# A metaformer block on one core: weights loaded by themselves, a first group in halves, uses placed one place later, scaling moved, and a last norm in four pieces

## What is computed

```python
x = x + conv_ref(_ln_c(x), w1, b1, w2, b2, w3, b3)
t = x.reshape(16, 1024, 128)
t = t + ffn_ref(_ln_t(t), W_gat, att_src, att_dst, ..., edge_index)
# conv_ref(A): three scans, each rewrites channels of A in place
#   4 steps:  A[..., 32 i : 32 i + 32] = conv1x1(A, w1) + b1;      then relu
#   4 steps:  A[..., 32 i : 32 i + 32] = conv3x3(A, w2) + b2;      then relu
#   128 steps: A[..., i] = conv1x1(A, w3) + b3;                    returns A + its input
# ffn_ref: h = x @ W_gat; attention of the nodes over 524,288 edges and its softmax give each
#   token scores; the best two of four experts (gelu networks) are summed with softmax weights
```

## Time and profile before

| | us |
|---|---|
| median of 3 runs | 2232.84 (2232.25 to 2235.68) |
| the profiled execution | 2235.35 |
| its span in the trace | 2233.7 |
| busy: PE, DVE, ACT, POOL | 1096.8, 1750.7, 772.6, 1183.2 |
| DVE busy in 75 to 470 | 387.65 of 395 |
| DVE busy in 550 to 575 | 1.40 of 25 |

### The profile page before, as it was taken

The page is one execution under the profiler, slowest core; times in us unless marked ns, Lnnn a source line. Parts: engine busy times, 40 slices in busy tenths (PEclk is TensorE's granted clock), DMA queues, the critical chain, the costliest instruction groups (busy, mean ns, idle before and its releaser), DMA issues. The chain is left out here.

```text
span 2233.7 us, 17018 instructions
## 1 busy us (share of the span) xinstructions
PE 1096.8 (49%) x4914; PEld 492.8 (22%) x4914; DVE 1750.7 (78%) x3468; ACT 772.6 (35%) x1293; POOL 1183.2 (53%) x1167
## 2 busy tenths in 40 slices
PE   3886887688678899301601243332424242415230
PEld 1223343333454333100200021111102020202010
DVE  5999999998649999999383555868685859595868
ACT  4663854635245555200300133222323131313121
POOL 2000000000047777777776777777777777777760
PEclk9898877878569999755855676676767575757665
DMA  8301131021455222211231234352524342524251
GB/s 290 134 1 39 38 8 38 1 8 39 45 43 99 73 73 71 52 15 41 76 45 13 39 104 123 74 165 62 174 64 156 83 156 68 171 67 157 67 147 56
DMA packets 142649, 177.40 MB, mean 79 GB/s; under 512 B 64154, under 2 KB 115292, under 8 KB 132956
## 3 DMA queue, kind: packets, MB, share of 16 engines
q1 hardware_dynamic: 86988, 88.84, 14.4%
q0 software_dynamic: 40768, 42.44, 12.0%
q10 hardware_dynamic: 14800, 45.04, 5.2%
HBM read 99.82 MB, written 76.40 MB: 79 GB/s over the span
## 5 line engine op out<-in xcount | busy, mean ns | idle before, releaser
L534 POOL DMA_INDIRECT KC<-node_dram,KB x1026 | 1051.3, 1025 | 939.9 <-DMA node_dram<-node_out 627.5
L757 PE MATMUL hidden_out<-XT,W 128*128 128x512 f32 x512 | 291.9, 677 | 552.3 <-ACT ARENA_A L977 551.4
L762 PE MATMUL hidden_out<-ARENA_A,W 128*128 128x512 f32 x512 | 267.2, 648 | 24.9 <-ACT ARENA_A L977 24.9
L977 ACT ACTIVATE ARENA_A<-hidden_out,b1c 128x512 f32<-128x512 f32 x256 | 174.2, 687 | 246.1 <-PE hidden_out L757 245.5
L757 PEld LDWEIGHTS hidden_out<-XT,W 128*128 128x128 f32 x512 | 98.9, 214 | 702.5 <-ACT ARENA_A L977 581.2
L1052 ACT ACTIVATE TA<-KB 128x320 f32<-128x320 f32 x64 | 26.0, 438 | 425.6 <-DVE KB L1705 425.5
L1695 DVE TENSOR_TENSOR KB<-KC,MB 128x320 f32<-128x320 f32 x66 | 29.2, 483 | 181.5 <-DMA KC<-payload,slot_idx 180.8
L1867 DVE SCALAR_TENSOR_TENSOR XG<-XT,KB,XG 128x128 f32<-128x128 f32 x512 | 144.3, 347 | 12.2 <-DMA XT<-ye_dram 8.5
L980 ACT ACTIVATE ARENA_A<-hidden_out,b2c 128x512 f32<-128x512 f32 x128 | 87.9, 687 | 188.0 <-PE hidden_out L762 188.0
L1711 DVE TENSOR_TENSOR KA<-KC,TA 128x1280 f32<-128x1280 f32 x66 | 95.2, 1484 | 57.9 <-ACT TA L1052 56.9
L762 PEld LDWEIGHTS hidden_out<-ARENA_A,W 128*128 128x128 f32 x512 | 98.2, 206 | 182.9 <-ACT ARENA_A L977 103.3
(11 more groups left out here) (407 smaller groups left out, 2151.2 us busy)
## 6 DMA issues: line engine op xcount, KB each, us to landing
ye_dram<-ARENA_D ACTq DMA_DIRECT2D x32, 1024.0 KB, 4.0
XT<-ye_dram SPq DMA_DIRECT2D x32, 1024.0 KB, 13.2
KC<-node_dram,KB POOLq DMA_INDIRECT x1026, 2.5
payload<-XT SPq DMA_DIRECT2D x1, 11520.0 KB
payload<-KC SPq DMA_DIRECT2D x115, 90.0 KB, 1.9
XG<-x_dram SPq DMA_DIRECT2D x32, 256.0 KB, 10.9
out_dram<-XG ACTq DMA_DIRECT2D x32, 256.0 KB, 2.9
KA<-in_L_ffn_edge_index_dram SPq DMA_DIRECT2D x1, 2048.0 KB, 9.1
```

What stands on the lines that cost most here:

```text
L534: pool.indirect_dma_start(row_buf[h][:, t, :], None, node_dram, bass.IndirectOffsetOnAxis(ap=KB[:, col:col + 1].bitcast(I32), axis=0)).the ...
L757: last = pe.matmul(PF[i % 2][:, :], W1[:, m // 2, (m % 2) * P:(m % 2) * P + P], XT[:, n * CHUNK:(n + 1) * CHUNK], start=True, stop=True)
L762: last = pe.matmul(PF[i % 2][:, :], W2[:, 2 * m + kk, :], HH[:, 2 * m + kk, :], start=kk == 0, stop=kk == 1)
L977: act.activation(HH[:, m, :], PF[i % 2][:, :], ACT.Gelu, bias=b1c[:, m:m + 1]).then_inc(S["hid_out"], 1)
```

## The change

- **Loads.** The three weights of the composition (`comp_in`) and the eight weights of the 3x3 and third scans (`conv_in`) are issued by ACT at its start, on semaphores of their own. SP issues x of group 0 in two halves, x of group 1, the edges, x of group 2, and the other 12 weights last. ACT runs one square root on a constant before it has work.
- **Halves at the start.** Statistics, root and scales of group 0 go in two halves (`STATS1`). The composition on DVE stands between pairs of `bn_stats` of the first half (`between`). The rest of the small weights moves behind the statistics of group 1 (`later_weights`) and behind the keys (`gat_weights`).
- **One place behind.** On PE the products (`use_chunk`) of a place's transposed chunks no longer follow their transposes; they stand at the head of the next place, ahead of its `step3`. On ACT the `chunk_out`s move with them (`pending_out` at the head of `place_work`).
- **Scaling for the residual.** L848 leaves `norm` and becomes `keep`: for group 0 all 8 chunks stand behind the first norms of group 1, for a later group 4 chunks behind each of its first two `relu`.
- **Last norm in four pieces.** Statistics, root, scales and norm of group 3 go by two chunks (`STATS2`). On PE the last four `step3` stand in pairs between the transposes and products of the pieces.

```diff
+STATS1 = [(0, 0, 4), (0, 4, 8)] + [(g, 0, 8) for g in range(1, GROUPS)]
+STATS2 = [(g, 0, 8) for g in range(GROUPS - 1)] + [(GROUPS - 1, c, c + 2) for c in range(0, 8, 2)]
...
-            move_x(0, x_groups[0], x_in, False)
+            x_first = XG[:, :].rearrange("p (t c) -> p t c", c=C)
+            for h in range(2):
+                tiles = slice(h * TILES // 2, (h + 1) * TILES // 2)
+                sp.dma_start(x_first[:, tiles, :], x_groups[0][:, tiles, :]).then_inc(x_first_in[h], 16)
+            move_x(1, x_groups[1], x_in, False)
+            edge_rows = edge_index.rearrange("a (p f) -> a p f", p=P)
+            sp.dma_start(KA[:, :].bitcast(I32), edge_rows[0]).then_inc(S["edges_in"], 16)
+            sp.dma_start(KB[:, :].bitcast(I32), edge_rows[1]).then_inc(S["edges_in"], 16)
...
+            move_x(2, x_groups[2], x_in, False)
             for dst, src in loads:
                 sp.dma_start(dst, src, allow_slow_non_contiguous=True).then_inc(S["weights_in"], 16)
-            assert len(loads) == N_WEIGHTS - 1
-            edge_rows = edge_index.rearrange("a (p f) -> a p f", p=P)
-            sp.dma_start(KA[:, :].bitcast(I32), edge_rows[0]).then_inc(S["edges_in"], 16)
-            sp.dma_start(KB[:, :].bitcast(I32), edge_rows[1]).then_inc(S["edges_in"], 16)
-            for g in (1, 2):
-                move_x(g, x_groups[g], x_in, False)
...
-            pe.wait_ge(S["weights_in"], 16 * (N_WEIGHTS - 1))
+            pe.wait_ge(S["comp_in"], 16 * N_COMP)
...
-            transposed, used = iter(range(NORMS)), iter(range(NORMS))
-
-            def norm_chunks(count):
+            transposed, pending = iter(range(NORMS)), []
+
+            def transposes(count):
 
                 for n in islice(transposed, count):
                     transpose_chunk(n)
-                    if NORM_ORDER[n] not in ((1, 0, 0), (1, 2, 0), (1, 3, 0), (2, 2, 0), (2, 3, 0), (1, 1, 0)):
-                        use_chunk(next(used))
-
-            def last_chunk():
-
-                use_chunk(next(used))
-
-            norm_chunks(CHUNKS)
-            last_chunk()
+                    pending.append(n)
+
+            def use_pending(count=NORMS):
+
+                for _ in range(min(count, len(pending))):
+                    use_chunk(pending.pop(0))
+
+            for c in range(CHUNKS):
+                transposes(1)
+                if c == 1:
+                    pe.wait_ge(S["comp_dve"], 8)
+                if c:
+                    use_pending(1)
+            use_pending()
+            pe.wait_ge(S["conv_in"], 16 * N_CONV)
             for g in range(GROUPS):
                 chunks = iter(range(CHUNKS))
+                if g == 1:
+                    pe.wait_ge(S["weights_in"], 16 * N_WEIGHTS)
+                    pe.wait_ge(S["comp_dve"], 9)
                 for place in range(8):
                     conv_half(g, place // 2, place % 2)
-                    if place == 0 and g >= 2:
-                        last_chunk()
+                    use_pending()
                     for c in islice(chunks, STEP3_FILL[g][place]):
                         step3(g - 1, c)
-                    norm_chunks(NORM_FILL[g][place])
+                    transposes(NORM_FILL[g][place])
                 if g == 0:
-                    last_chunk()
-            last_chunk()
-            for c in range(CHUNKS):
+                    use_pending()
+            use_pending()
+            for c in range(4):
                 step3(GROUPS - 1, c)
-            norm_chunks(CHUNKS)
-            last_chunk()
+            for c in range(0, CHUNKS, 2):
+                transposes(2)
+                if c + 4 < CHUNKS:
+                    step3(GROUPS - 1, c + 4)
+                    step3(GROUPS - 1, c + 5)
+                use_pending()
...
+                act.dma_start(dst, src, allow_slow_non_contiguous=True).then_inc(S["comp_in"], 16)
...
+                act.dma_start(dst, src, allow_slow_non_contiguous=True).then_inc(S["conv_in"], 16)
             act.wait_ge(S["consts"], 10)
+            act.activation(std2[:, :], ones[:, 0:TILES], ACT.Sqrt)
...
-                if kind == 1:
-                    for t in range(TPC):
-                        tt = TPC * c + t
-                        last = act.activation(x_tile(g, tt), x_tile(g, tt), ACT.Identity,
-                                              scale=scale1x[g % 2][:, tt:tt + 1], bias=shift[:, tt:tt + 1])
-                    last.then_inc(S["xres_ready"], 1)
+
+            def keep(g, c):
+
+                for t in range(TPC):
+                    tt = TPC * c + t
+                    last = act.activation(x_tile(g, tt), x_tile(g, tt), ACT.Identity,
+                                          scale=scale1x[g % 2][:, tt:tt + 1], bias=shift1[g % 2][:, tt:tt + 1])
+                last.then_inc(S["xres_ready"], 1)
...
+            def place_work(g, place):
+
+                pending_out()
+                first = sum(sum(row) for row in NORM_FILL[:g]) + CHUNKS + sum(NORM_FILL[g][:place])
+                for n in range(first, first + NORM_FILL[g][place]):
+                    copies(1)
+                    kind, h, c = NORM_ORDER[n]
+                    if c < CHUNKS - 2 or c == CHUNKS - 1 and (kind, h) in ((1, 2), (1, 3)):
+                        norms(n + 3)
...
+                    if g and i < 2:
+                        for c in range(i * CHUNKS // 2, (i + 1) * CHUNKS // 2):
+                            keep(g, c)
...
-            last_chunk()
+                        place_work(g, 2 * i + 2)
+            pending_out()
             root2(GROUPS - 1)
-            first_norms(2, GROUPS - 1)
-            norm_chunks(CHUNKS)
-            last_chunk()
+            for k in range(GROUPS - 1, len(STATS2)):
+                norms(norm_at[(2, GROUPS - 1, 0)] + 2 * (k - GROUPS + 2))
+                copies(2)
+                if k + 1 < len(STATS2):
+                    root2(k + 1)
+                pending_out()
 
...
+            def token_stats(k, between=iter(())):
+
+                g, first, end = STATS1[k]
+                if g:
+                    dve.wait_ge(x_in[g], 16 * len(x_parts[g]))
+                else:
...
+                    if t % 2:
+                        next(between, None)
...
+                    k = part_of(STATS2, g, c)
+                    if c + 1 == STATS2[k][2]:
+                        link(last)
+                        variances(STATS2, k, mean_var2, std2, 1e-5, "var2_ready")
+                    if k >= GROUPS and c == STATS2[k][1]:
+                        scales2(k - 1)
                     sort_steps(STEPS_AFTER[g][c])
-                link(last)
...
-            token_stats(0)
+            small = small_weights()
+            token_stats(0, small)
             scales1(0)
-            small_weights()
-            token_stats(1)
+            token_stats(1, small)
+            scales1(1)
+            token_stats(2)
+            later_weights()
             keys = make_keys()
             next(keys)
-            scales1(1)
+            scales1(2)
             next(keys)
-            token_stats(2)
+            gat_weights()
+            token_stats(3)
             sort_steps(15)
-            scales1(2)
+            scales1(3)
             sort_steps(4)
...
-            scales2(3)
+            scales2(len(STATS2) - 1)
```

More of the change, by code:

```diff
@@ L118, with part_of @@
 ROUND_MAGIC = 12582912.0
+STATS1 = [(0, 0, 4), (0, 4, 8)] + [(g, 0, 8) for g in range(1, GROUPS)]
+STATS2 = [(g, 0, 8) for g in range(GROUPS - 1)] + [(GROUPS - 1, c, c + 2) for c in range(0, 8, 2)]
+def part_of(parts, g, c):
+    return next(k for k, (h, first, end) in enumerate(parts) if h == g and first <= c < end)
 def trips_before(n):
@@ L947, in _ @@
                     first_norms(1, 1)
-                if g >= 2:
-                    last_chunk()
+                    for c in range(CHUNKS):
+                        keep(0, c)
                 for i in range(4):
+                    if i == 0:
+                        place_work(g, 0)
                     if i < 3:
@@ L1093, in token_stats, with variances @@
                 link(last)
[L1094 to L1098 removed]
+                variances(STATS1, k, mean_var1, std1, 1e-6, "var1_ready")
+            def variances(parts, k, mean_var, std, eps, ready):
+                g, first, end = parts[k]
+                for t in range(first * TPC, end * TPC):
                     last = dve.bn_aggr(mean_var[:, t, :], bn[:, t, :])
                 link(last)
[L1101 removed]
@@ L1426, in _ @@
             scales2(0)
-            token_stats(3)
+            token_stats(4)
             sort_steps(18)
-            scales1(3)
+            scales1(4)
             sort_steps(7)
```

144 lines of the change are left out of this document (80 added, 64 removed).

## The result

The changed kernel takes 2252.77 us (2252.02 to 2254.07) beside 2232.89 on the same chip: a ratio of 1.0082 (95% interval 1.007 to 1.0094), 19.9 slower. The forecast was 2233.1, no change, with a range to 2242; the time lies beyond it, on the side to which I gave 0.25. Its profiled execution took 2254.07, with a span of 2252.4.

What follows compares the result with a forecast made beforehand. POOL's gathers were taken to bound the kernel, so its start sets the end: the end part 9.3 later less 9.0 gained at the start gives +0.3, from 2232.84 to 2233.1, range 2223 to 2242.

Steps and rivals of the forecast that it cites:

- What bounds the kernel: POOL's gathers run without pause once node rows are stored, so the end moves one for one with POOL's start.
- The start: DVE begins at 9.05 and loses composition waits, so group 2's statistics begin about 9.0 earlier, bounds 7.5 to 10.
- Rival 3: At the start, the first half of the loads comes late, PE getting comp_in at 16 or later: up to 2242; chance 0.15.
- The middle: Up to group 2's residuals, moved scaling and later products leave PE ready ahead of DVE, with 10 spare before.
- The prediction's last sentence: If PE reaches group 2's residuals later than DVE, near 472, the start's gain was eaten and the sum fails.
- the orders of groups 1 and 2 cost or save up to 2: New work orders in the middle groups change PE's readiness for residuals by at most 2.
- Rival 4: The end stacks worse: indices end last or ACT's group 3 scaling delays a rewrite in 481 to 564: 2240; chance 0.10.
- From 481 to the last read-out: Group 3's first residual comes 6.2 later, its last 17.9 later; 8.6 come back, so the last read-out is 9.3 later.
- the 1.45: Between 481 and 564, the last half of the convolution starts and ends 1.45 earlier, as products move behind it.
- Rival 1: The last norm's four pieces pay: waits do not stack, read-out near 616, time 2211; chance 0.06.
- Rival 2: PE's work at the end gets the 2.4 GHz clock, saving about 9: 2224; chance 0.17 including its middle ground, 2228.
- just hidden: Behind the last read-out, window indices are ready at 662.1 against 662.7 needed, so POOL does not wait for them.

Runs made afterwards that it cites:

- run 12: Against the original: changed start and scaling, products beside transposes until the last place, pieces with step3 0 to 5 first, POOL's second memset beside group 1's statistics: 2222.85, 0.9952.
- run 5: Changed kernel with at most two products left pending for the next place: 2239.40, 1.0023 of the original.
- run 6: Changed kernel with each four residual scalings moved behind the next place's work on ACT: 2251.45, 1.0081 of the original.
- run 7: Changed kernel with all eight residual scalings of a later group behind its first relu, where no products are pending: 2242.61, 1.0038 of the original.
- run 11: Against the original: changed start and scaling, products beside transposes until the last place, memset held until composition done, pieces with step3 0 to 5 first: 2223.66, 0.9952.

## Why the prediction was wrong

**What bounds the kernel: right.** In every run the end moved with POOL's start and its first window: from that window to the end the traces take 1579.7 to 1584.4 (before 1580.3, the changed kernel 1584.3, which is the 4 left open below).

**The start: mechanism right, size off.** I had 9.0 at the statistics of group 2 and it was 6.1. Of the missing 2.9, 2.6 are the one copy that took 2.81; in run 12, where nothing of the start is stretched, the statistics of group 2 are 8.7 early.

That the copy would be held the trace of before could not show, since DVE then started at 11.60 and ran statistics alone until that memset had ended at 12.84. On the loads I took the trace's side and counted nothing, and that was right: the DMA engines moved 201 GB/s in the first 12 (190 before), and PE's first composition step started at 9.01, released by POOL's memset. The rule of the Trainium skill, "DMA: Bandwidth & Descriptors", section "Issuing engines are not separate DMA queues", that a second issuer saves only issue time, does not speak against this. The gain came from what the waits ask for and from issue time, not from bandwidth: in the trace of before SP's issuing of the 23 loads took from 1.93 to 20.30, the last one's from 19.87, with PE waiting for it to 23.95; SP was through with the composition's three at 8.41, and in the changed kernel ACT is at 2.30. How the gain divides between a wait for three loads only and a second issuer no run shows. Rival 3 (the first half comes late) fell with the start at 9.01. Of the 6.1 only 5.3 were left at the first residual: the first four exchanges of the sort took 9.2 in place of 8.3; why is open.

**The middle: the step that failed.** The prediction's last sentence names this way to fail, PE later than DVE to the residuals (there those of group 2; it was those of group 1). But ahead of it I wrote that the later products and the moved scaling leave PE ready ahead of DVE, since "the orders of groups 1 and 2 cost or save up to 2". The four bank waits cost PE 40, of which its slack covered only part; DVE lost 2.1 at a root and 5.4 at the residuals of group 1, and came to those of group 2 3.1 later than before. I had the rule in hand (a use waits for what lies in its bank two uses earlier) and applied it only to the last place, where the third product also stands. Runs 5, 6 and 7 show it in the middle: with two pending the waits vanish, and they are as long as what ACT has ahead of the read-out. Rival 4 came nearest, but for its place: I had looked for the scaling's damage in group 3, behind 481.

**From 481 to the last read-out: right in mechanism, and in part by luck in the sum.** Timeline of the changed kernel:

```profile
574.29 3.45 PE L690 MATMUL MB<-node_w,XT 128*128 128x24 f32 x16
...
575.16 4.50 ACT L949 ACTIVATE ARENA_A<-hidden_out,cb 32x1024 f32<-32x1024 f32 x4
...
579.68 0.39 ACT L918 ACTIVATE node_out<-MB 128x96 f32<-128x96 f32 x2
...
580.08 1.87 PE L690 MATMUL MB<-node_w,XT 128*128 128x24 f32 x8 [2.33 <-ACT node_out L918]
...
584.58 0.69 DVE L1205 TENSOR_TENSOR KB<-KB,MB 128x512 f32<-128x512 f32 x1 [30.21 <-issue]
```

The third product waits for the read-out behind the relu, as in the prediction. But the first residual of group 3 is 100.2 behind that of group 2, 7.9 more than before, where I had 6.2. Nearly all of that difference is the 1.45 by which I let the last half of the convolution end earlier. It did not: the work behind it (the three products) starts 83.5 after the first residual of group 2, and in the trace of before (a transpose) 83.3 after it.

```profile
567.83 2.86 PE L690 MATMUL MB<-node_w,XT 128*128 128x24 f32 x24
```

```profile
564.53 0.65 PE L671 MATMUL TA<-ident,ARENA_Y 128*128 128x128 f32 x4
```

The first row is the changed kernel's, the second that of before. First residual to last: 39.2, forecast 39.9, before 28.2. Last residual to the read-out's end: 18.5, forecast 19.3, before 27.9. These two, 0.7 and 0.8 short, cancel most of the 1.7, so that 9.6 came out beside 9.3. Rival 1 (the pieces pay) fell in this order, for the reason given against it; run 11 shows that it was the order. Rival 2 fell: the granted clock was 0.71 in 560 to 600 and 0.53 in 600 to 650, against 0.62 and 0.50, still nearer to the lower level; in short stretches it was near the upper one (0.89 in 585 to 590, 0.98 in 603 to 606, a `step3` of 1.16 in place of 2.08).

**Behind the last read-out.** I called the indices "just hidden" with 0.6 to spare; they were not, and POOL waited 3.47. The first gather took 1.35 in place of 2.80, so net the first window lost 2.1 on the first gather. Two more us appear between the first window and the gather of the chain, and no wait holds them: the 1,017 gathers behind the first nine took 1043.1 in all, with idle time of 309.9, and 1041.0 with 310.0 before. Why they took 2 ns longer each, and where the 1.9 behind them come from, stays open.

## What to carry to other kernels

Count the buffers that a delayed use holds: with two banks, a third pending result blocks its engine until another engine has read out the first, and the wait is as long as what that engine still has ahead of that read-out; check every place at which the pattern occurs, not only the one on the path at the end. Splitting a last stage pays only when the engine's order lets the early pieces run without holding up what feeds the later ones. And a gain at the start is worth what is left of it at each point where two engines meet: read those points one by one.

## What the runs showed of the hardware

While POOL's memset of 128 x 4624 ran, a DVE copy of 32 x 129 took 2.81 and not 0.22, ending 0.08 after the memset, and an addition on 128 x 16 took 2.02 and not 0.17, ending 0.02 after it; 32 statistics beside a memset of the same size took 6.29 against 6.28. The Trainium skill, "GPSIMD Engine Reference", section "1. Specifications", says that GpSimd's interfaces to SBUF are shared with VectorE, with contention for VectorE's instructions in a 2-port perf mode or with two inputs from SBUF. The traces agree in that some instructions stop until the memset ends and others lose nothing. In which mode the copy and the addition ran no trace shows, and no DVE instruction with two inputs ran under a memset, so what one would lose no run here shows.
